# An attention block's order on TensorE and VectorE: the second unit of maxima goes behind the projection, and VectorE's remainder goes ahead of the turned sum

## The reference

```python
# 2 batches, 2048 rows, 256 columns; 16 heads of 64; causal
hn = layernorm(h) * gamma + beta
q, k, v = hn @ Wq + bq, hn @ Wk + bk, hn @ Wv + bv
q, k = rope(q), rope(k)          # x * cos + neg_half(x) * sin
attn = softmax(where(mask, q @ k.T / 8, -inf))
x = layernorm(h + (attn @ v) @ Wo + bo + h)
x = layernorm(x + (silu(x @ Wg.T) * (x @ Wu.T)) @ Wd.T)
```

## Time and profile before

| | us |
|---|---|
| median of 3 runs | 2259.03 |
| lowest and highest | 2257.0, 2262.46 |
| the profiled execution | 2253.5 |
| its span in the trace | 2251.6 |
| busy in it: TensorE, VectorE, GpSimd, ScalarE | 2076.9, 1594.7, 1387.8, 911.3 |

### The profile page before, as it was taken

One profiled execution on the slowest core, in us unless ns is written; L12 is line 12 of the kernel. 1 busy time (PEld: TensorE's weight loads), 2 busy tenths in 40 slices (PEclk: granted clock), 3 DMA queues, 4 the chain that ended last, 5 costly groups with the idle time before them and its releaser, 6 DMA issues.

```text
span 2251.6 us, 37497 instructions
## 1 busy us (share of the span) xinstructions
PE 2076.9 (92%) x14720; PEld 1301.5 (58%) x14720; DVE 1594.7 (71%) x2262; ACT 911.3 (40%) x1245; POOL 1387.8 (62%) x1204
## 2 busy tenths in 40 slices
PE   6779999999999999889999999999999989889997
PEld 5445555555555555455555555555555544789996
DVE  7576868686878787657777777777777774556654
ACT  4424344434343444334444344443334444334432
POOL 1447777777787777457777777777777879000000
PEclk9889999999999999899999999999999999999999
DMA  6311212121212022122121212121211130221300
GB/s 221 118 29 38 62 38 62 39 62 38 57 27 68 26 55 71 48 68 77 39 62 39 61 39 62 38 62 29 53 31 50 33 122 23 91 95 64 105 16 29
DMA packets 116149, 132.16 MB, mean 59 GB/s; under 512 B 15248, under 2 KB 71184, under 8 KB 115728
## 3 DMA queue, kind: packets, MB, share of 16 engines
q1 hardware_dynamic: 115984, 129.92, 19.3%
HBM read 56.47 MB, written 39.85 MB: 43 GB/s over the span
## 4 chain that ended last, share of the span: by engine, by line
PE 60%; DVE 24%; issue 6%; DMA 4%; SPq 3%; ACT 1%; POOL 1%; DVEq 0%; ACTq 0%
PE o_ps L1230 14%; DVE mpart L828 8%; PE m_ps L1175 8%; PE s_ps L1196 4%; DMA rot<-qr 4%; PE s_ps L1200 4%; PE s_ps L1198 3%; PE s_ps L1202 3%; SPq L381 3%; PE x_ps L1130 3%; DVE qk L871 3%; DVE qc L866 2%; PE x_ps L1132 2%; PE x_ps L1131 2%; PE gu_ps L1130 2%
## 5 line engine op out<-in xcount | busy, mean ns | idle before, releaser
L537 POOL TENSOR_TENSOR acc<-acc,pt 128x512 f32<-128x512 f32 (+3 forms) x1024 | 1189.4, 1194 | 206.2 <-ACT pt L586 205.6
L828 DVE TENSOR_REDUCE mpart<-m_ps 128x2 f32<-128x1024 f32 (+2 forms) x576 | 625.4, 1086 | 362.7 <-PE m_ps L1175 237.1
L586 ACT ACTIVATE pt<-s_ps 128x1024 f32<-128x1024 f32 (+3 forms) x640 | 545.7, 896 | 716.3 <-PE s_ps L1202 412.1
L1230 PE MATMUL o_ps<-pt,v 128*64 128x512 f32 (+3 forms) x2560 | 558.7, 559 | 0.0
L1175 PE MATMUL m_ps<-qk 64*128 64x512 f32 (+3 forms) x1280 | 288.7, 447 | 105.0 <-DVE mpart L828 97.8
L1175 PEld LDWEIGHTS m_ps<-qk 64*128 64x128 f32 x1280 | 122.1, 187 | 387.5 <-DVE mpart L828 185.8
L532 POOL TENSOR_TENSOR acc<-pt 128x512 f32<-128x512 f32 (+1 forms) x128 | 165.0, 1310 | 227.6 <-ACT pt L586 227.6
L1230 PEld LDWEIGHTS o_ps<-pt,v 128*64 128x64 f32 x2560 | 159.4, 139 | 247.9 <-issue 232.2
L1196 PE MATMUL s_ps<-qk 64*128 64x512 f32 (+3 forms) x1280 | 250.1, 387 | 0.0
L1200 PE MATMUL s_ps<-qk 64*128 64x512 f32 (+3 forms) x1280 | 236.5, 365 | 0.0
L1198 PE MATMUL s_ps<-qk 64*128 64x512 f32 (+3 forms) x1280 | 235.8, 364 | 0.0
(11 more groups left out here) (165 smaller groups left out, 2884.2 us busy)
## 6 DMA issues: line engine op xcount, KB each, us to landing
rot<-qr SPq DMA_DIRECT2D x512, 64.0 KB, 2.0
attn<-o_sum SPq DMA_DIRECT2D x64, 256.0 KB, 2.3
o_raw<-attn SPq DMA_DIRECT2D x8, 2048.0 KB, 8.9
v<-v_far SPq DMA_DIRECT2D x16, 768.0 KB, 5.2
v_far<-v_part SPq DMA_DIRECT2D x48, 256.0 KB, 2.0
w_raw<-in_wqkv SPq DMA_DIRECT2D x34, 128.0 KB, 5.0
v_far<-v SPq DMA_DIRECT2D x16, 256.0 KB, 2.5
v<-v_far SPq DMA_DIRECT2D x16, 256.0 KB, 4.7
```

The source lines that it names most:

```text
L537: nc.gpsimd.tensor_tensor(sums, sums, probs, ALU.add).then_inc(summed, 1)
L586: nc.scalar.activation(pt[:, u % SLOTS, :, q0:NB], s_ps[:, two:two + 2, q0:NB], ACT.Exp, scale=SCALE)\
L828: nc.vector.tensor_reduce(dst, m_ps[:, :, 0:w], AX.X, ALU.max, negate=True).then_inc(maxed, 1)
L1230: last = nc.tensor.matmul(o_ps[rows, q0:NB], v[par][:, j, rows], pt[:, u % SLOTS, a, q0:NB], start=(j == 0), stop=(j == n - 1), skip_group ...
```

## The change

On TensorE, in all pairs but the first, the second unit of maxima of a group moves behind what the group does with `x_ps` (transposes, projection or piece of v) and stands ahead of `weigh`. In groups without such a use (2, 6, 12, 0, and those of absent v pieces) it stays where it was, right behind the scores. On VectorE, in all pairs but the first, `piece_lo` stands between the two maxima instead of at the group's end. In all pairs `turned_sum` goes to the end, behind the division. In the first pair both maxima stay ahead and `piece_lo` follows them.

```diff
--- before.py
+++ after.py
@@ -912,10 +912,16 @@
                         turn_sums(it - 1 if g == 1 else it, ended)
                     if g - 1 in PIECE and kind is not LAST:
                         products(it + 1, *PIECE[g - 1], 1 - par, 2)
-                    for m in group_maxima(kind, g):
+                    ms = group_maxima(kind, g)
+                    late = 1 if kind is not FIRST else len(ms)
+                    for m in ms[:late]:
                         maximum(it, m) if m < NM else maximum(it + 1, m - NM)
                     if turns and kind is FIRST:
                         spread(it + 1 if g == NG - 1 else it, TURN_M[g])
+                    if g - 2 in PIECE and kind is not LAST:
+                        piece_lo(it + 1, *PIECE[g - 2], 1 - par)
+                    for m in ms[late:]:
+                        maximum(it, m) if m < NM else maximum(it + 1, m - NM)
                     if g == 1 and kind is not LAST:
                         weights(it + 1)
                     if (it, g) in WV_SPLIT:
@@ -923,13 +929,11 @@
                     if g in HN_SPLIT and kind is SWITCH:
                         for k in range(KC):
                             next_lo(HN_SPLIT[g], k)
-                    if g - 1 in PIECE and kind is not LAST:
-                        turned_sum(it + 1, *PIECE[g - 1])
                     if ended is not None:
                         invert(it - 1 if g == 1 else it, ended)
                         divide(it - 1 if g == 1 else it, ended)
-                    if g - 2 in PIECE and kind is not LAST:
-                        piece_lo(it + 1, *PIECE[g - 2], 1 - par)
+                    if g - 1 in PIECE and kind is not LAST:
+                        turned_sum(it + 1, *PIECE[g - 1])
                     if g in FFN_SPLIT and kind is LAST:
                         split_ffn(FFN_SPLIT[g])
                     if g in OUT_SPLIT and kind is LAST:
@@ -1272,15 +1276,17 @@
                     ms = group_maxima(kind, g)
                     us = group_units(g)
 
-                    for i, m in enumerate(ms):
-                        pe.wait_ge(maxed, it * NM + m)
-                        maxima(it, par, m) if m < NM else maxima(it + 1, 1 - par, m - NM)
-                        if i == 0:
-                            scores(kind, it, par, us[0])
-                            scores(kind, it, par, us[1])
-                    if len(ms) == 0:
-                        scores(kind, it, par, us[0])
-                        scores(kind, it, par, us[1])
+                    def some_maxima(which):
+                        for m in which:
+                            pe.wait_ge(maxed, it * NM + m)
+                            maxima(it, par, m) if m < NM else maxima(it + 1, 1 - par, m - NM)
+
+
+                    late = 1 if kind is not FIRST else len(ms)
+                    some_maxima(ms[:1])
+                    scores(kind, it, par, us[0])
+                    scores(kind, it, par, us[1])
+                    some_maxima(ms[1:late])
                     if g in TURN_M and (g != NG - 1 or nxt):
                         shared_free(g, 0)
                         turn_maxima(it + 1 if g == NG - 1 else it, TURN_M[g])
@@ -1290,6 +1296,7 @@
                         shared_free(g, 0)
                         project(it + 1, *PIECE[g], 2)
                     values_piece(g, 0)
+                    some_maxima(ms[late:])
                     if g > 0:
                         weigh(kind, it, par, g - 1)
                     elif kind is not FIRST:
```

## The result

| | median us | lowest, highest | runs |
|---|---|---|---|
| before | 2257.0 | 2252.38, 2262.46 | 9 |
| changed | 2266.87 | 2261.53, 2277.79 | 9 |

The ratio is 1.0046 with a 95% interval of 1.0025 to 1.0066. The changed kernel is slower, by some 10 us. I had forecast slower by 27. The sign was right and the size was not.

A forecast was written before the change was run, and what follows sets the result against it. TensorE bounds the kernel (busy 2076.9 of 2251.6 us), with VectorE setting the pace in gapless stretches. Group terms gave 1.9 us a pair, times 14 about 27, on 2259: 2286 us; forecast 2264 to 2304 (0.60), range 2256 to 2312.

The forecast's parts named there:

- Groups 1 and 2, +0.42: Transposes ahead delay group 1's second maxima; VectorE's chain without slack makes TensorE 0.42 us late by group 2.
- Groups 3 and 4, +0.45, and 7 and 8, +0.45: Later second maxima delay VectorE's division and second product; the projections of groups 4 and 8 wait, losing 0.45 us each.
- Group 5, +0.56: Transposes fill 0.59 us of the old wait, but VectorE's late chain takes more; `weigh` is 1.43 us late in all.
- Groups 10 to 13, −0.33: Group 10 gains 0.43 us as the projection covers a late reduction; groups 11 to 13 lose 0.1, remainder delaying group 13.
- Group 19, +0.3: `spread` and the reduction come later, so second maxima wait some 1.0 us; less 0.59 for transposes ahead, +0.3.
- Pairs without v: Same terms with +1.2 in group 9, −1.84 in group 10, +1.0 in group 14, smaller group 19 loss: about 1.85 us.
- The sum of a middle pair, +1.9: All group terms of a middle pair together: a loss of 1.85 us, taken as 1.9, SWITCH pair included.
- the 111.5 to 113 that were to show the mechanism: Sign in the new trace: pair 11 takes 111.5 to 113 us, from 110.24; under 110 would be wrong.
- 14 x 1.9: Whole kernel: 13 middle pairs and the SWITCH pair lose 1.9 us each, 26.6 us; first and last pair nothing.
- rival 4: More half-speed clock after TensorE's waits: once more a pair costs 16 us, 2302; its part inside the forecast's 0.60.
- Rival 3 (long remainders): Two remainders a pair take 1.77 instead of 0.7 us ahead of an awaited reduction: 2317; with all above 2304, 0.15.
- Rival 1: Cover wins: second maxima nearly always find their predecessor reduced; 2170, or 2215 if `x_ps` takes half back; faster 0.16.

The follow-up runs named there:

- runs 3 and 10: Changed kernel with VectorE's division also between the reductions in groups 3, 7, 13: 2225.21 us; changed kernel with second maxima ahead of the projection in groups 3, 7: 2226.82 us.
- Run 2: The changed kernel's VectorE order with TensorE's order of the kernel before: 2213.18 us, ratio 0.9801 to the kernel before.
- Run 7: VectorE's new order; TensorE's second maxima moved behind the piece of q, k or v only in groups 15 to 18: 2230.22 us, ratio 0.9881 to before.

## Why the prediction was right and wrong

- **Groups 1 and 2, +0.42.** Right: +0.41.
- **Groups 3 and 4, +0.45, and 7 and 8, +0.45.** The mechanism was right (runs 3 and 10) and the size too small: +1.18 and +1.17 in groups 4 and 8. With groups 3 and 7 that is 1.35 and 1.37, some 0.9 more than forecast each: in groups 3 and 4 the division's product took 1.62 us where it stands now, against 0.92, and 0.2 is the term left out below. I kept the old length for a moved operation with two inputs in SBUF. The Trainium skill (SBUF — State Buffer, Who interferes with whom) says that such an operation and GpSimd's exclude each other; 0.92 and 1.62 for one instruction fit that (the rows are in the last section), and I had applied it to the remainder alone.
- **Group 5, +0.56.** Wrong in sign: −0.69. The spread took 0.16 instead of 0.98 us and the turned sum 1.10 instead of 1.52, the same effect the other way round. So the transposes waited 0.34 us for the second product and the second maxima 0.47 for the reduction, 0.81 together where 1.57 stood before. The shorter operations are luck: no term of the sum had them. Over groups 1 to 8 the sum was +1.88 forecast and +2.44 measured.
- **Groups 10 to 13, −0.33.** Measured −1.27. I had priced the remainder's move in group 12 as a loss of 0.6 ahead of group 13. Run 2 shows it to be a gain of 0.85 there (0.27 of it comes back in group 14), because the gap that it fills was idle.
- **Left out: 0.2 us in each group with a projection.** Groups 3, 7, 9 and 14 to 17 rise by 0.17 to 0.21 and group 18 by 0.11 without any wait: 1.5 us a pair with v. No term of the sum had it.
- **Group 19, +0.3.** Measured +0.24.
- **Pairs without v.** The forecast +1.2 in group 9, −1.84 in group 10 and +1.0 in group 14 were measured as +1.28, −1.91 and +1.26 in pair 14. Group 19, forecast as a small loss, was a gain of 1.33. The sum of 1.9 is right and that term is not.
- **The sum of a middle pair, +1.9.** Measured +2.5 and +1.9 in undisturbed pairs. It came out near because a loss left out (0.2 a group) and a gain left out (VectorE's order, 1.4 to 2.7 us a pair in run 2) stood against each other; that is luck. Pair 11 took 112.8, inside the 111.5 to 113 that were to show the mechanism. For the SWITCH pair 1.9 was too little: it took 4.3 more, with 6.8 us less at half speed, so its order costs 7 to 8.
- **From the pair to the whole: the step that failed.** I took 14 x 1.9 as the result and the clock as a rival that could only add. By the undisturbed pairs the change costs 7 x 2.5 + 6 x 1.9 = 29 us in the middle pairs; 6.7 were measured. So the clock, put at nothing in the sum, gave back most of what the order cost. The difference, 22, is close to what the kernel before lost in its 11 half-speed stretches (half of 41.0 is 20.5) and the changed one doesn't. The estimate over all executions agrees for the whole kernel: +35 at full clock, −22 of half speed. So the order was priced some 8 us too low, most of that in the SWITCH pair, and the clock's gain was left at nothing. The prediction had the row for it, 0.53 of the clock behind the wait of 1.57 us in group 5, saw that the change cuts this wait in two, and priced rival 4 only as a cost.
- **The rivals.** None came in as written. Rival 3 (long remainders) didn't occur as priced: L871 fell from 1009 to 884 ns in the mean, and the one of 1.8 us in group 10 of pairs without v was there before; only that of group 19 there grew, from 0.68 to 1.39 us. Rival 1's mechanism isn't there either, but half the change, VectorE's, is a gain of 42 us that no rival named. The uncertainty section says that the reductions agree in every row; only one was shown. The whole trace bears it out: all 448 of this shape take 1.18 to 1.23 us, before and in the changed kernel.

## What to carry to other kernels

Split a change by engine before pricing it: here one half gains 42 us, the other costs 65, and the whole, +10, shows neither. Put work into a wait only if nothing that waits for its neighbour is on another engine's full stretch: behind transposes the move gave 1% on top of VectorE's 2%, behind projections, whose bank VectorE must empty first, it cost. And when a wait of TensorE is shortened or cut in two, count the half-speed stretches that begin there, by the records of the granted clock, as a term of the sum.

## What the runs showed of the hardware

- Putting the second maxima (row-tiled, 64 rows) between the projection (128 rows) and `weigh`, instead of behind the row-tiled scores, adds one more change of tiling and 0.2 us a group with no wait in it: 1390.58 to 1394.71 before from the first maxima of group 3 to `weigh`, 4.13 us, and 1401.21 to 1405.52 in the changed kernel, 4.31. Run 7 shows the same 0.2 in groups 15 to 17. The Trainium skill (TensorEngine Tiling (Array Packing), Key Properties) says that changing the tiling mode drains TensorE; the sizes agree with that, but no run changed the tiling alone.
- Waits of 1.5 to 2.5 us in group 5 were followed by 1.2 GHz in 7 of 13 middle pairs before. In the changed kernel, with the wait cut in two (0.34 and 0.47 us, at most 1.41 and 0.47), none was. Four more pairs of products that nobody needs, in that wait and in that of group 10, made the kernel 12 us faster. What decides between two pairs with the same wait is open.
- In pair 11 the same copy (`spread`, L842) took 0.98 us ahead of the transposes of group 5 before and 0.16 in the changed kernel, and the same product of the division 0.92 and 1.62. Only the order differs. Together VectorE and GpSimd were busy 83 us less in the changed kernel for the same instructions. The rows of the two engines show who waits: in pair 11 of the changed kernel GpSimd's addition began first and the product took long; in pair 2 the product began 0.03 us ahead, took 0.69, and GpSimd's addition took 1.81 us instead of 1.29. Both in the changed kernel, pair 11 and then pair 2:

```profile
1407.58 1.29 POOL L537 TENSOR_TENSOR acc<-acc,pt 128x512 f32<-128x512 f32 x1
1407.80 1.62 DVE L890 TENSOR_TENSOR o_sum<-o_sum,r_t 128x512 f32<-128x512 f32 x1
...
354.70 0.69 DVE L890 TENSOR_TENSOR o_sum<-o_sum,r_t 128x512 f32<-128x512 f32 x1
354.73 1.81 POOL L537 TENSOR_TENSOR acc<-acc,pt 128x512 f32<-128x512 f32 x1
```

- Pairs 3, 8, 9 and 10 of the changed kernel take 0.4 to 1.8 us more than pair 2 (112.6) at full clock. In pairs 3 and 10 the turned sum of group 4 waited 2.01 and 1.82 us for the DMA into `rot`, in pair 11 0.53, and the transposes of group 5 then waited 1.41 and 1.31 us instead of 0.34. Still open are why those DMAs land late, and what lengthens pairs 8 and 9.
